# A mixture-of-experts layer: every third expert block transposed by the DMA engines instead of TensorE

## The reference

```python
x = x + layernorm(x) @ (weight * block_mask).T          # the projection
x2 = layernorm(x)
top = top_k(x2 @ W_gate + b_gate, 2)                    # two experts per token
y = relu(x2 @ W_e[e] + b_e[e]) for the two experts e    # mean over the two
x = x + y
```

## Time and profile before

| | |
|---|---|
| median of 3 runs | 691.74 us (691.38 to 692.23) |
| profiled execution | 691.82 us, span 689.8 us |
| PE busy | 672.6 us, 98% of the span, 3551 matmuls |
| PEld / DVE / ACT / POOL busy | 79% / 44% / 42% / 40% |
| DMA, mean | 177 GB/s |

### The profile page before, as it was taken

How to read it: one execution, slowest core, us unless ns; L and a number is a source line. 1 busy time by engine, 2 the same in 40 slices (tenths; PEclk the granted TensorE clock), 3 DMA queues, 4 the chain that set the end, 5 groups by cost and what they waited for, 6 DMA issues and landing times.

```text
span 689.8 us, 11078 instructions
## 1 busy us (share of the span) xinstructions
PE 672.6 (98%) x3551; PEld 548.1 (79%) x3551; DVE 301.0 (44%) x549; ACT 289.5 (42%) x421; POOL 278.6 (40%) x252
## 2 busy tenths in 40 slices
PE   7999999999999999999999999999999999999993
PEld 5667777888787888888888888888888888888882
DVE  5886688877985552450622610541533420000000
ACT  7875544455743343333334343434333333334330
POOL 2023122135661366363645443453535362534330
PEclk9999999999999999999999999999999999999998
DMA  8992635497552588684784855694875854322223
GB/s 354 407 393 65 278 120 185 168 323 258 187 204 83 184 219 219 177 241 126 205 251 100 255 144 115 176 245 100 232 224 114 260 109 93 56 41 43 49 37 55
DMA packets 34756, 122.39 MB, mean 177 GB/s; under 512 B 5008, under 2 KB 5008, under 8 KB 34704
## 3 DMA queue, kind: packets, MB, share of 16 engines
q1 hardware_dynamic: 23472, 84.46, 33.4%
q0 software_dynamic: 11232, 37.23, 26.8%
HBM read 87.59 MB, written 37.75 MB: 182 GB/s over the span
## 4 chain that ended last, share of the span: by engine, by line
PE 96%; DMA 1%; ACT 1%; SPq 0%; issue 0%; POOLq 0%; DVE 0%; ACTq 0%
PE psO L443 83%; PE psT L733 5%; PE psT L476 2%; PE psT L443 2%; PE psO L476 1%; PE psG L549 1%; DMA xb<-data_t 1%; PE psS L530 1%; PE psT L517 0%; PE psT L561 0%; POOLq L49 0%; PE psT L538 0%; DVE w_stage L1312 0%; ACT xT L823 0%; ACT wT L837 0%
## 5 line engine op out<-in xcount | busy, mean ns | idle before, releaser
L443 PE MATMUL psO<-slots,xT 128*128 (+1 forms) x1872 | 435.9, 392 | 0.0
L443 PEld LDWEIGHTS psO<-slots,xT 128*128 128x128 f32 x1872 | 348.2, 188 | 70.6
L1637 POOL DMA_INDIRECT rows_out<-xb,tok_of x37 | 63.4, 1714 | 222.9 <-ACT xb L1050 216.7
L1050 ACT ACTIVATE xb<-psO 128x512 f32<-128x512 f32 x78 | 46.6, 598 | 254.2 <-PE psO L443 254.2
L443 PE MATMUL psO<-wT,xT 128*128 128x512 f32 x624 | 152.3, 397 | 0.8 <-ACT psO L881 0.8
L1300 DVE CAST slots<-raw 128x1024 fp32r<-128x1024 f32 x56 | 51.8, 925 | 197.8 <-PE psO L443 109.3
L443 PEld LDWEIGHTS psO<-wT,xT 128*128 128x128 f32 x624 | 114.3, 188 | 26.0 <-issue 2.7
L1631 POOL TENSOR_TENSOR xT<-x2T,xT 128x1024 fp32r<-128x1024 f32 x38 | 99.3, 2613 | 18.4 <-ACT x2T L1029 18.3
L1302 DVE TENSOR_TENSOR slots<-raw,slots 128x1024 fp32r<-128x1024 f32 x56 | 72.8, 1299 | 1.9
L990 ACT ACTIVATE psO<-bias_slot 128x512 f32 (+1 forms) x78 | 47.0, 602 | 35.8 <-ACT xb L1050 16.9
L1024 ACT ACTIVATE xT<-psT 128x1024 fp32r<-128x1024 f32 x38 | 38.4, 1011 | 7.7 <-PE psT L733 7.7
(11 more groups left out here) (225 smaller groups left out, 507.6 us busy)
## 6 DMA issues: line engine op xcount, KB each, us to landing
raw<-L_ffn_W_e SPq DMA_DIRECT2D x56, 512.0 KB
x_rows<-x SPq DMA_DIRECT2D x16, 512.0 KB, 4.0
xb<-data_t SPq DMA_DIRECT2D x12, 512.0 KB, 4.1
mask_stage<-mask_blocks SPq DMA_DIRECT2D x8, 512.0 KB, 10.4
w_stage<-weight_t SPq DMA_DIRECT2D x8, 512.0 KB, 11.2
row_stage<-L_attn_weight SPq DMA_DIRECT2D x8, 512.0 KB, 12.0
xr<-L_attn_data SPq DMA_DIRECT2D x8, 512.0 KB, 5.6
rows_out<-xr SPq DMA_DIRECT2D x8, 512.0 KB, 3.0
```

Of the source, the lines that this page charges most:

```text
L443: last = eng.matmul(psum, xT[:, p, a, kt, :], moving(b, kt), start=(i == 0 and kt == 0 and not seeded), stop=(i == len(PASSES) - 1 and kt ...
L1050: eng.activation(xb[:, b % 2, n * HALF:(n + 1) * HALF], psO[:, n, :], ACT.Relu, scale=1.0 / TOP_K).then_inc(c_out, 1)
L1637: eng.indirect_dma_start(out, bass.IndirectOffsetOnAxis(ap=tok_col(b), axis=0), xb[:, b % 2, :], None, bounds_check=N_TOK + P - 1, compute ...
```

## The change

The planes of x2 are new: each float32 is two 16-bit halves, and a second scratch tensor `x2_planes` holds for every token the 1024 low halves and then the 1024 high ones. In the projection ScalarE makes them, tile by tile, in one instruction over 2048 16-bit elements (`split_planes`), and SyncE stores them. In the expert phase blocks 5, 8, ..., 38 (12 blocks) are gathered from `x2_planes` instead, transposed by a DMA issued from ScalarE's queue (`turn_rows`), and put together again by ScalarE (`join_rows`). The other blocks stay as they were, with a ring of three buffers instead of four; the fourth is the buffer of the DMA blocks. `planes` lies over `raw[0]`, `turned` over `xr[1]`.

```diff
+        x2_planes = nc.dram_tensor("x2_planes", (N_TOK, 2 * D), U16, kind="Internal").ap()
+        planes = at("planes", [P, 2, D], U16, raw_offset)
+        turned = at("turned", [P, 2 * KT, P], U16, xr_offset + D * 4)
         def rows_of(b, cols=slice(0, D)):
+            ring = 3 if by_dma(b) else turns_of_pe(b) % 3
-        HI0_AT = {10: (0,), 11: (1, 2), 12: (3, 4), 13: (5, 6), 14: (7,)}
+        HI0_AT = {10: (0,), 11: (1, 2), 12: (3,), 13: (4, 5), 14: (6,), 15: (7,)}
+        def by_dma(b):
+            return b > EARLY + 2 and b % 3 == 2
...
 # SyncE
+            def store_planes(t):
+                eng.wait_ge(c_planes, t + 1)
+                eng.dma_start(x2_planes[t * P:(t + 1) * P, :], planes[:]...).then_inc(l_planes, 16)
+            store_x2(1); store_planes(0); store_x1(2); store_x2(2); store_planes(1)
             for i in range(FIRST, NB + 1):
                 store_x2(i - 1)
+                store_planes(i - 2)
+            store_planes(NB - 1)
-            eng.wait_ge(s_spare, 16)
+            eng.wait_ge(l_planes, 16 * NB)          # ahead of the weight loads of place 1
...
 # TensorE
-                if b > EARLY and b + 1 < N_BLOCKS:
+                if b > EARLY and b + 1 < N_BLOCKS and not by_dma(b + 1):
                     transpose_rows(b + 1)
-                eng.wait_ge(c_rhi, 2 * b - 1)
+                eng.wait_ge(c_rhi, 2 * b if by_dma(b) else 2 * b - 1)
...
 # ScalarE
+            def split_planes(t):
+                eng.wait_ge(c_ln2, t + 1)
+                if t == 0:
+                    eng.wait_ge(s_spare, 16)
+                else:
+                    eng.wait_ge(l_planes, 16 * t)
+                eng.activation(planes[:], x2[:, t % 2, :].bitcast(U16).rearrange("p (d h) -> p h d", h=2), ACT.Copy).then_inc(c_planes, 1)
             gate_out(7)
+            split_planes(5)
             mean1(8)
             square1(8)
             seed_mean(8, 0)
+            split_planes(6)
...
                 norm2(i - 1)                        # loop of i, 8 to 16
+                if i == NB:
+                    split_planes(i - 1)
...
                     seed_mean(i + 1, 0)
+                if i < NB:
+                    split_planes(i - 1)
+            def turn_rows(b):
+                eng.wait_ge(l_gather[3], 16 * turns_of_dma(b))
...
+                    eng.wait_ge(c_rhi, 2 * (b - 3))
+                eng.dma_start_transpose(turned[:], rows_of(b).bitcast(U16)).then_inc(l_turn, 16)
+            def join_rows(b):
+                eng.wait_ge(l_turn, 16 * turns_of_dma(b))
+                eng.wait_ge(c_rlo, b - 1)
+                eng.activation(x2T[:].bitcast(U16).rearrange("p k (t h) -> p h (k t)", h=2),
+                               turned[:].rearrange("p (h k) t -> p h (k t)", h=2), ACT.Copy).then_inc(c_rhi, 1)
+                eng.wait_ge(c_rhi, 2 * b - 1)
+                eng.wait_ge(c_half, NH * b)
+                eng.activation(xT[:, b % 2, HI, :, :], x2T[:], ACT.Copy).then_inc(c_rhi, 1)
...
+                    if n == 0 and b + 3 < N_BLOCKS and by_dma(b + 3):
+                        turn_rows(b + 3)            # after half 0 is moved out and seeded
+                    if n == 0 and b + 1 < N_BLOCKS and by_dma(b + 1):
+                        join_rows(b + 1)
...
 # GpSimd
+            eng.wait_ge(c_planes, NB)
+            eng.memset(x2[:, 1, :], 0.0).then_inc(c_clear, 1)
             for b in range(1, N_BLOCKS):
-                if b + 1 < N_BLOCKS:
+                if b + 1 < N_BLOCKS and not by_dma(b + 1):
                     rows_lo(b + 1)
-                if b + 3 < N_BLOCKS:
+                if b + 3 < N_BLOCKS and not by_dma(b + 3):
                     gather_rows(b + 3)
+                if b + 4 < N_BLOCKS and by_dma(b + 4):
+                    gather_rows(b + 4)              # waits for the DMA transpose before it
+                if b + 1 < N_BLOCKS and by_dma(b + 1):
+                    rows_lo(b + 1)
                 add_rows(b)
```

More of the change, by code:

```diff
@@ L10 @@
 I32 = mybir.dt.int32
+U16 = mybir.dt.uint16
 ALU = mybir.AluOpType
@@ L197, in build @@
         through = sb("through", [P, N_EXP], I32)
-        assert cursor[0] <= xr_offset + 2 * D * 4 and end <= nc.sbuf_usable_end
+        assert cursor[0] <= xr_offset + D * 4 and end <= nc.sbuf_usable_end
+        turned = at("turned", [P, 2 * KT, P], U16, xr_offset + D * 4)
         def rows_of(b, cols=slice(0, D)):
-            return (rows_a[:, cols], rows_b[:, cols], x2[:, 0, cols], x2[:, 1, cols])[b % 4]
+            ring = 3 if by_dma(b) else turns_of_pe(b) % 3
+            return (rows_a[:, cols], rows_b[:, cols], x2[:, 0, cols], x2[:, 1, cols])[ring]
         def resid(t, cols=slice(0, D)):
@@ L292, in build, with turns_of_pe, turns_of_dma @@
         c_first, c_pick = sem("c_first"), sem("c_pick")
+        c_planes, c_clear, l_planes, l_turn = sem("c_planes"), sem("c_clear"), sem("l_planes"), sem("l_turn")
         ST, TOP, PLACE, HOT, RS1, RS2, GATES = 3, 11, 4, 3, 2, 4, 5
         FIRST_KNOWN, FIRST_TOK = 4, 15
-        HI0_AT = {10: (0,), 11: (1, 2), 12: (3, 4), 13: (5, 6), 14: (7,)}
+        HI0_AT = {10: (0,), 11: (1, 2), 12: (3,), 13: (4, 5), 14: (6,), 15: (7,)}
         GATHER_AT = NB - 2
+        def by_dma(b):
+            return b > EARLY + 2 and b % 3 == 2
+        def turns_of_pe(b):
+            return len([c for c in range(1, b + 1) if not by_dma(c)])
+        def turns_of_dma(b):
+            return len([c for c in range(1, b + 1) if by_dma(c)])
         def turn_bank(b):
@@ L359, in store_x2 @@
                 eng.dma_start(x2_rows[t * P:(t + 1) * P, :], x2[:, t % 2, :]).then_inc(l_x2[t % 2], 16)
+            def store_planes(t):
+                eng.wait_ge(c_planes, t + 1)
+                eng.dma_start(x2_planes[t * P:(t + 1) * P, :], planes[:].rearrange("p h d -> p (h d)")).then_inc(l_planes, 16)
             for c in range(KT):
@@ L389, in _ @@
             load_x(7)
-            for t in (1, 2):
-                store_x1(t)
-                store_x2(t)
+            store_x1(1)
+            store_x2(1)
+            store_planes(0)
+            store_x1(2)
+            store_x2(2)
+            store_planes(1)
             def expert_of(place):
@@ L955, in _ @@
             square1(6)
+            split_planes(0)
             norm2(2)
             gate_out(4)
+            split_planes(1)
             norm2(3)
@@ L963, in _ @@
             seed_mean(6, 0)
+            split_planes(3)
             x_hi(7)
@@ L1043, in _ @@
             for b in range(N_BLOCKS):
-                if 1 < b + 1 < N_BLOCKS and b != 1:
+                if 1 < b + 1 < N_BLOCKS and b != 1 and not by_dma(b + 1):
                     rows_hi(b + 1)
```

30 lines of the change are left out of this document (24 added, 6 removed).

## The result

The changed kernel takes 697.55 us (median of 8 runs, 695.68 to 702.65) beside 691.99 us of the kernel before on the same chip (691.11 to 694.55). The ratio is 1.0088 with a 95% interval of 1.0070 to 1.0105: slower by 0.9%, where 684.5 was forecast. The profiled run took 696.94 us with a span of 695.2.

The account below looks back on a forecast made before the run. TensorE, busy 672.6 of 689.8 us, was taken as the bound. -11.5 + 0.3 + 1.3 + 1.0 + 1.7 = -7.2 us from 691.82 gave 684.6, as median 684.5; range 680.5 to 716.

Parts of the forecast that it names:

- -11.5 for the transposes: Expert blocks: 12 blocks without TensorE transposes, 0.96 us each, take 11.5 us off TensorE's program.
- +0.3 for the join: Expert blocks: join on ScalarE, taken at 1.83 us, is hidden except at block 38, costing 0.3 us.
- spare microsecond: Expert blocks: 1.0 us between the high copy's end and TensorE asking for it, after transposing the next block.
- bound of 11 us for a slow join: Expert blocks: a join of 3.7 us would cost 0.9 us a block, 11 us in all.
- 0 for issue and landing of the transposing transfer: Expert blocks: DMA transpose from ScalarE's queue is issued and lands within the free time, costing 0 us.
- Rival 1: Expert blocks, slower: the transpose's issue holds ScalarE beyond 8.1 us; 10 us would give 707; chance 0.28.
- X and T: DMA transpose: time the issue holds ScalarE, 8.1 us free, and time until the transfer lands, 22.6 us free.
- +1.3 for the seed of tile 8: Projection: the split of tile 5 delays the seed of tile 8 on ScalarE, so TensorE waits 1.3 us.
- +1.0 for the other tiles: Projection, loop and hand-written part: waits from splits and planes' landing, taken about 6 us, cost 1.0; bounds 0 and 15.
- +1.7 for the change-over: Projection to experts: high copy and split of tile 14 delay block 0's seed; TensorE waits 1.7 us, range 0.8 to 5.
- Weights of place 1: Expert start: loads begin about 233.6 instead of 224.98; last split at about 275, hidden with 5 us or more spare.
- rival 2: Projection, no gain: planes landing 8.5 us after issue cost six loop tiles 1 us each, change-over 1.5; 692; chance 0.14.

Follow-up runs that it names:

- e6: The changed kernel with second planes buffer, seeds ahead of splits, rows loaded before planes' stores, join first, first weight's high copies in old places: 681.56 us, ratio 0.9854.
- e9: e6 with every second block from block 5 on gathered as planes, 17 instead of 12: 676.65 us, ratio 0.9780.
- e2: Expert part alone: the kernel before with 12 DMA blocks gathered from plain rows, no planes split or stored, output wrong: 684.41 us, ratio 0.9904.
- e5: e2 with the join moved to the head of ScalarE's iteration, ahead of the move-out: 681.57 us, ratio 0.9859.
- e12: e6 with the join back in its late place, behind the seed of half 0: 684.64 us, ratio 0.9889.
- e8: e2 with a plain DMA copy of the same bytes in place of the transposing transfer, output wrong: 683.40 us, ratio 0.9870.
- e7: The changed kernel with 40 useless matmuls on TensorE ahead of the wait for block 0's first seed: 694.61 us, ratio 1.0053.
- e10: The changed kernel with a second buffer for the planes and nothing else changed: 689.98 us, ratio 1.0004.
- e11: e6 with one buffer for the planes instead of two, its orders kept: 688.54 us, ratio 0.9948.
- e3: The changed kernel with block 0's first seed put ahead of the split of tile 14: 692.33 us, ratio 1.0022.

## Why the prediction was wrong

The forecast was 7.2 us less; the kernel takes 5.6 us more (697.55 beside 691.99). The view of the bound was right: what TensorE waited less or more, and what its clock fell, is what the marks and spans of these kernels show. The terms, as the prediction put them:

- **-11.5 for the transposes.** Right in kind, a little large: 12 blocks bring 10.4 us in e6 (440.7 - 430.3), 0.87 each, and the 17 of e9 bring 15.1, 0.89 each. The difference of 0.96 was taken between a time from start to start (11.77) and half a length (21.63 / 2). From start to start, two blocks of e6 with one set of transposes between them instead of two take 22.66 us (289.79 to 312.45), and two blocks of the kernel before 23.57: 0.91.
- **+0.3 for the join.** Wrong, and one of the three steps that failed. Its length was taken from contiguous copies and is 2.51 us, inside the bounds of 1.01 and 3.7. By the prediction's own clock this still fits in its spare microsecond. What failed is that one undisturbed block stood for all twelve. The join had been put behind a move-out and a seed that wait for others: in a block with a small gap the seed came 0.7 us later than in that one, and once ScalarE waited 6.68 us for the output rows. Block 38, for which the 0.3 stood, shows 0.73 by itself. The late place costs 2.8 us between the medians of e2 and e5, 3.1 between e12 and e6 (3.1 and 2.4 by the ratios), 4.6 in the profiled run of after (435.0 against e6's 430.3). The bound of 11 us for a slow join held, the value didn't.
- **0 for issue and landing of the transposing transfer.** Right: 1.3 to 3.5 us against 8.1, and 4.3 to 17.2 against 22.6. Rival 1, with 0.28, had the direction right, since the issue of a plain copy of the same bytes takes 0.48 us (e8), but not the size. Only X and T were looked at, not what the transfer does to others, for which e8 shows no clear price.
- **+1.3 for the seed of tile 8.** Right: 1.24.
- **+1.0 for the other tiles.** Wrong: about 4.6, the rest of the +5.9 up to block 0. The prediction followed the split through ScalarE's queue and the planes' landing through their buffer, tile by tile in the loop, where nothing was lost (85.21 us from the first half of tile 8 to the last half of the projection before, 85.23 after). It did not follow the store of the planes through SyncE's queue in the part written out by hand, where a load of rows stands behind it. The load that goes 6 us late accounts for the waits of 2.4 and 1.0 us. Of the remaining 1.2, TensorE waits 0.6 longer for wT at the start of the kernel; that wait differs from run to run (1.6 to 2.9 us in these kernels), and the rest isn't located.
- **+1.7 for the change-over.** Wrong: 5.3. The place, the order and the issue were right (214.7 forecast, which with the 5.9 us of delay is 220.6; it was 220.56). The landing was taken at 3.5 us and was 5.6, within the 2.6 to 7 allowed for; the wait then is 2.9, inside the range of 0.8 to 5. The clock was not in the sum at all, and gave 1.6 more; a wait on blk_tok 0.5.
- **Weights of place 1.** Hidden, as said; the load started at 239.52, and no wait of a block on a weight appears in this trace (that of e7 has one, in a later place).

So three steps failed, and they took about as much each: 3.6 us in the hand-written part, 3.6 at the change-over and 4.3 in the join. That 697.55 lies inside the stated 680.5 to 716 is luck: the upper part of that range stood for rival 1, an issue that holds ScalarE, which did not come.

What the projection took was rival 2's subject, and its chance was 0.14. It named one mechanism (landing in the loop) where the trace shows two others (a store ahead of a load, a landing at the change-over). Most of that hangs on the single buffer, which e10 and e11 price at 7.6 and 7.0 us (5.8 and 6.5 by the ratios). In e10 it takes all but 0.7 of the change-over, and 2.7 of the 5.9 before it, of which the rest is the seed of tile 8 (1.24) and the order on SyncE (waits of 0.7 and 1.0). The change-over loses its time only where the single buffer and the split ahead of the seed come together: e3, with one buffer, mends it by the order alone (15.12 us from mark to mark beside 15.14 in e10). These two losses are why the kernel was slower: with the second buffer it can't be told from before (1.0004, 0.9963 to 1.0045). The late join is the larger part of why it was not faster. With both mended and the orders too, the gain is 10.5 us (692.06 - 681.56), more than the 7.2 forecast, since the mended kernel pays none of the costs.

Of the Trainium skill's two figures on the landing, that of DMA: Bandwidth & Descriptors, Latency and other measured facts, an estimate of 2 us for the half megabyte, is too low beside the measured 4.3 at best, and that of VectorE: DVE Perf Modes, The three transpose paths, 21 us for 16 squares in a row, too high beside a median of 5.6: the times of the 16 squares of a transfer did not add up. Neither would have changed the sum.

## What to carry to other kernels

When work is added to an engine in a stage, its own time there is rarely the cost: follow each new buffer through one whole round (fill, issue, landing, next fill) at the tightest place of every stage, and each new transfer through the queue that issues it, up to the first load that stands behind it. A wait of TensorE can cost more than its length, when the granted clock falls after it. A producer of the next block's input belongs at the head of the in-order queue, ahead of instructions that wait for others. One steady block shows whether it fits, not what it costs when a transfer is late.

## What was not expected of the hardware

- A copy of 2048 16-bit elements on ScalarE takes 1.91 us when it reads with a stride and writes in a row (the split), and 2.51 us when it reads in a row and writes with a stride (the join).
- The transposing transfers move 6.29 MB in 24,960 packets, 252 bytes each on average, where a plain copy of the same bytes needs 1,728. Their issue holds the queue 1.3 to 3.5 us, up to 5.0 in e5, where the plain copy's takes 0.48.
- A VectorE operation on 128x8 integers that takes 0.16 us elsewhere took up to 2.37 us while GpSimd ran a subtraction of 128x1024. In the timeline of the kernel after both start within 0.05 us of each other, and the short one ends with the long one:

```profile
157.75 2.40 POOL L1700 TENSOR_TENSOR slots<-w_stage,slots 128x1024 fp32r<-128x1024 f32 x1 [4.38 <-ACT slots L1053]
...
157.80 2.37 DVE L1242 TENSOR_TENSOR pos_r<-pos_i,low_bits 128x8 int32<-128x8 int32 x1
```
